# Attention scalars of a graph network: columns per group, or rows per pair of groups

## What is computed

```python
x = layernorm(x + gcn(x))                       # two graph convolutions, 128 -> 256 -> 128
xs, xd = x[src], x[dst]
att = sigmoid(xs @ W_att[:d] + xd @ W_att[d:] + b_att)
messages = (xs @ W_msg + b_msg) * att
aggregated = segment_sum(messages, dst, num_segments=num_nodes)
h = gru(aggregated, x)                          # W_ih, W_hh; then a batch norm over the nodes
return layernorm(x + h)
```

## Time and profile before

| | |
|---|---|
| median of 3 runs | 1699.89 us (1697.44 to 1700.52) |
| span of the profiled execution, all that is shown of its time | 1805.3 us |
| busy in it: PE, PEld | 1517.2 us (84%), 1054.6 us (58%) |
| busy in it: DVE, ACT, POOL | 1403.1 us (78%), 1172.9 us (65%), 986.4 us (55%) |
| HBM | 270.98 MB read, 175.92 MB written |

### The profile page before, as it was taken

One profiled execution on the slowest core, in us unless ns is written; L12 is line 12 of the kernel. 1 busy time (PEld: TensorE's weight loads), 2 busy tenths in 40 slices (PEclk: granted clock), 3 DMA queues, 4 the chain that ended last, 5 costly groups with the idle time before them and its releaser, 6 DMA issues.

```text
span 1805.3 us, 35081 instructions
## 1 busy us (share of the span) xinstructions
PE 1517.2 (84%) x7736; PEld 1054.6 (58%) x7736; DVE 1403.1 (78%) x4685; ACT 1172.9 (65%) x2896; POOL 986.4 (55%) x1014
## 2 busy tenths in 40 slices
PE   6303899999999938888888889999999999997764
PEld 3101677777777737767777776455555555555553
DVE  7827688888888847777677774788888888888897
ACT  6873455555555516666666665777777777776999
POOL 5002666666666356666656663666666666634443
PEclk9656999999999979999989998999999999999998
DMA  8898799988888737888766665877864445446997
GB/s 300 296 334 322 249 327 323 330 281 273 271 273 272 249 116 259 268 273 270 231 212 217 217 214 193 248 240 240 243 208 142 138 139 143 141 145 239 405 405 284
DMA packets 244030, 448.07 MB, mean 248 GB/s; under 512 B 39256, under 2 KB 40978, under 8 KB 243936
## 3 DMA queue, kind: packets, MB, share of 16 engines
q1 hardware_dynamic: 215248, 388.16, 62.3%
q0 software_dynamic: 28688, 58.89, 13.1%
HBM read 270.98 MB, written 175.92 MB: 248 GB/s over the span
## 4 chain that ended last, share of the span: by engine, by line
PE 46%; DVE 17%; issue 13%; ACT 10%; another core or an unknown queue 3%; DVEq 2%; DMA 1%; POOL 1%; ACTq 0%; SPq 0%; POOLq 0%
PE bank L1515 5%; PE bank L1523 5%; PE bank L1618 5%; PE bank L1605 5%; PE bank L1611 5%; PE bank L1607 5%; PE bank L1603 5%; PE bank L1610 4%; ACT page L905 4%; DVE page L1231 3%; ACT page L1008 3%; DVE gath L1397 3%; PE bank L1505 2%; PE bank L1549 2%
## 5 line engine op out<-in xcount | busy, mean ns | idle before, releaser
L783 POOL DMA_INDIRECT gath<-MT,ROWI x294 | 319.2, 1086 | 203.2 <-PE bank L1618 111.7
L783 POOL DMA_INDIRECT gath<-XP,ROWI x294 | 286.8, 976 | 228.6 <-remote 85.1
L783 POOL DMA_INDIRECT gath<-G,ROWI x294 | 278.8, 948 | 193.4 <-PE bank L1549 72.8
L879 ACT ACTIVATE page<-bank,b_sb 128x512 f32<-128x512 f32 x196 | 124.3, 687 | 164.5 <-remote 116.5
L1523 PEld LDWEIGHTS bank<-w_sb,page 128*128 128x128 f32 x1568 | 191.5, 192 | 51.5 <-issue 50.8
L1549 PE MATMUL bank<-gath,onehot 128*128 128x128 f32 x1176 | 168.4, 295 | 62.8 <-issue 30.5
L1523 PE MATMUL bank<-w_sb,page 128*128 128x128 f32 x1568 | 192.4, 275 | 4.2 <-issue 2.5
L1515 PE MATMUL bank<-page,w_sb 128*128 128x512 f32 x392 | 191.1, 610 | 3.6 <-DVE page L1212 2.8
L1549 PEld LDWEIGHTS bank<-gath,onehot 128*128 128x128 f32 x1176 | 149.2, 203 | 69.3 <-issue 64.9
L887 ACT ACTIVATE page<-bank,DINV 128x128 f32<-128x128 f32 x392 | 112.3, 372 | 74.9 <-remote 57.0
L905 ACT ACTIVATE page<-page,st_m,st_r 128x128 f32<-128x128 f32 x384 | 156.8, 479 | 0.0
(11 more groups left out here) (226 smaller groups left out, 3382.5 us busy)
## 6 DMA issues: line engine op xcount, KB each, us to landing
page<-YT SPq DMA_DIRECT2D x196, 256.0 KB, 7.9
MT<-page SPq DMA_DIRECT2D x98, 260.0 KB
XP<-page SPq DMA_DIRECT2D x98, 256.0 KB, 3.0
page<-in_xT SPq DMA_DIRECT2D x98, 256.0 KB
page<-DQ SPq DMA_DIRECT2D x98, 256.0 KB
G<-page SPq DMA_DIRECT2D x98, 256.0 KB
OWN<-page SPq DMA_DIRECT2D x98, 256.0 KB
page<-OWN SPq DMA_DIRECT2D x98, 256.0 KB
```

Of the source, the lines that this page charges most:

```text
L783: nc.gpsimd.indirect_dma_start(gath[k][:, w, 0:width], None, rows, bass.IndirectOffsetOnAxis(ap=ROWI[:, at:at + 1], axis=0)).then_inc(land ...
L879: last = nc.scalar.activation(rows[k], bank[2 + 2 * k + h][:], ACT.Relu, bias=b1_sb[:, h:h + 1])
```

## The change

For each group one product with the vectors as the stationary side, into two of four rows of a bank: `watt_pair[0]` has the vectors in columns 0 and 2, `watt_pair[1]` in columns 1 and 3, zeros elsewhere, and the two products of a pair of groups add up. So rows 0 and 1 hold the first scalar of the pair's groups, rows 2 and 3 the second. ACT copies the four rows to `att_rows` (two pages). SP stores rows 2 and 3 to AD. PE multiplies four rows by four columns of the identity per tile: one plain product for the first tile, which starts the bank anew, and three in transpose mode. DVE adds the bias on the way into the two `n_m` pages. MT is stored one step later (lag 9), and HN before it. The table `AD_ALL` goes, with its transposes, copy and stores at the end of the stage, and the four late recurrent products follow each other.

The core of the diff:

```diff
+        watt_pair = [sb(f"watt_pair{u}", [P, 4]) for u in range(2)]
...
-        AD_ALL = DSQ
+        att_rows = pages[16:18]
...
+                if (g := group_of(8)) and not g.kept:
+                    wait(sp, n_hk, g.done())
+                    sp.dma_start(group_of_table(HN, g), n_h[g.slot(4)]).then_inc(h_st[g.slot(4)], 16)
+                if (g := group_of(8)) and g.c % 2:
+                    wait(sp, n_ad, g.pair())
+                    sp.dma_start(AD[bass.ds(g.i * g.unroll + (g.c - 1), 2)].rearrange("a j p -> a (j p)"),
+                                 att_rows[g.pair_slot()][2:4, :]).then_inc(ad_st[g.pair_slot()], 16)
+                if g := group_of(9):
                     k = g.slot(8)
-                    wait(sp, n_mc, g.done())
+                    wait(sp, n_mc, g.pair())
                     sp.dma_start(group_of_table(MT, g), n_m[k][:]).then_inc(n_mst[k], 16)
...
-            sp.wait_ge(n_ad, 1)
-            whole = len(AD_CHUNKS) - 1
-            sp.dma_start(ad_rows[0:whole * P, :].rearrange("(q p) c -> p q c", p=P),
-                         n_h[3][:, 0:whole * P].rearrange("p (q c) -> p q c", c=P)).then_inc(ad_st, 16)
-            sp.dma_start(ad_rows[whole * P:NT, :], n_h[3][0:AD_CHUNKS[-1], whole * P:GN]).then_inc(ad_st, 16)
...
             def norm(group_of):
+                if (g := group_of(7)) and g.c % 2:
+                    k = g.pair_slot()
+                    wait(act, n_mm, g.pair())
+                    wait(act, ad_st[k], g.pair_dma_freed())
+                    nc.scalar.activation(att_rows[k][0:4, :], bank[4 + k][0:4, :], ACT.Copy).then_inc(n_ad, 1)
...
-            wait_all_dmas(act, h_st, 1, FREE)
-            act.wait_ge(n_adt, 1)
-            nc.scalar.activation(n_h[3], bank[3][:], ACT.Copy).then_inc(n_ad, 1)
...
+            for u in range(2):
+                nc.vector.memset(watt_pair[u][:], 0.0)
...
+            for u in range(2):
+                nc.vector.tensor_copy(watt_pair[u][:].rearrange("p (s u) -> p s u", s=2)[:, :, u:u + 1], watt_sb[:].unsqueeze(2))
...
-                    wait(dve, n_mm, g.done())
-                    nc.vector.tensor_copy(AD_ALL[:, bass.ds(g.index * J, J)], both[:, :, 1:2].rearrange("p j a -> p (j a)"))
-                    nc.vector.tensor_tensor(by_tile(n_m[g.slot(8)][:])[:, :, D:DM], both,
-                                            batt_sb[:].unsqueeze(1).to_broadcast([P, J, 2]), ALU.add).then_inc(n_mc, 1)
+                if (g := group_of(8)) and g.c % 2:
+                    wait(dve, n_adt, g.pair())
+                    both = bank[4 + g.pair_slot()][:, 0:4 * J].rearrange("p (j s u) -> p j s u", j=J, s=2)
+                    for u in range(2):
+                        last = nc.vector.tensor_tensor(by_tile(n_m[(g.c - 1 + u) % 8][:])[:, :, D:DM],
+                                                       both[:, :, :, u:u + 1].rearrange("p j s u -> p j (s u)"),
+                                                       batt_sb[:].unsqueeze(1).to_broadcast([P, J, 2]), ALU.add)
+                    last.then_inc(n_mc, 1)
...
-                    wait(pe, n_mc, g.freed(2))
+                    u = g.c % 2
+                    if u == 0:
+                        wait(pe, n_mc, g.pair_freed())
+                    product = nc.tensor.matmul(bank[4 + g.pair_slot()][0:4, :], watt_pair[u][:], y, start=u == 0, stop=u == 1)
+                    if u:
+                        product.then_inc(n_mm, 1)
+                if (g := group_of(7)) and g.c % 2:
+                    k = g.pair_slot()
+                    wait(pe, n_ad, g.pair())
                     for j in range(J):
-                        last = nc.tensor.matmul(bank[4 + g.slot(2)][:, 2 * j:2 * j + 2], y[:, j * P:(j + 1) * P], watt_sb[:], start=True, stop=True)
-                    last.then_inc(n_mm, 1)
+                        last = nc.tensor.matmul(bank[4 + k][:, 4 * j:4 * j + 4], att_rows[k][0:4, j * P:(j + 1) * P], ident[0:4, 0:4],
+                                                is_transpose=j > 0, start=True, stop=True)
+                    last.then_inc(n_adt, 1)
```

More of the change, by code:

```diff
@@ L115, in pairs, with pair, pair_slot, pair_freed @@
         return self.i * (self.unroll // 2) + (self.c + 1) // 2
+    def pair(self):
+        return self.i * (self.unroll // 2) + self.c // 2 + 1
+    def pair_slot(self):
+        return self.c // 2 % 2
+    def pair_freed(self):
+        return self.pair() - 2
+    def pair_dma_freed(self):
+        return self.i * (16 * self.unroll // 4) + 16 * (self.c // 4)
     def dma(self, k, n=1):
@@ L161, in in_register, with run_pass @@
     return value if isinstance(value, int) else eng.to_reg(value)
-def run_pass(eng, step, lag, kept_only=False, unroll=U):
+def run_pass(eng, step, lag, kept_only=False, unroll=U, head=None):
     def at(i, u, kept=None):
@@ L172, in at @@
         return group_of
-    first, border, last = -(-(lag + unroll) // unroll), FREE // unroll, NG // unroll
+    first, border, last = head or -(-(lag + unroll) // unroll), FREE // unroll, NG // unroll
     if not kept_only:
@@ L665, in norm @@
                     sp.dma_start(group_of_table(YT, g), n_T[k]).then_inc(n_yst[k], 16)
-                if g := group_of(8):
+                if (g := group_of(8)) and not g.kept:
[6 more added lines that the diff above has]
+                if g := group_of(9):
                     k = g.slot(8)
-                    wait(sp, n_mc, g.done())
+                    wait(sp, n_mc, g.pair())
                     sp.dma_start(group_of_table(MT, g), n_m[k][:]).then_inc(n_mst[k], 16)
[L670 to L674, removed]
+            run_pass(sp, norm, 9, unroll=8, head=2)
             sp.wait_ge(n_zz, NG)
@@ L687, in stored @@
                 wait_all_dmas(sp, n_mst)
-                sp.wait_ge(ad_st, 32)
+                for u in range(2):
+                    sp.wait_ge(ad_st[u], 16 * len(range(u, NG // 2, 2)))
                 wait_all_dmas(sp, h_st, 1, FREE)
@@ L911, in norm @@
                     wait(act, n_yst[k], g.dma_freed(4))
-                    wait(act, n_mm, g.freed(4))
+                    wait(act, n_mm, g.pair() - 2)
                     nc.scalar.activation(n_T[k], bank[2 + g.slot(2)][:], ACT.Copy).then_inc(n_trc, 1)
@@ L926, in hidden @@
                 nc.scalar.activation(kept(g) if g.kept else n_h[k], bank[6 + g.slot(2)][:], ACT.Copy).then_inc(n_hk, 1)
[L928 to L931, removed]
-            wait_all_dmas(act, h_st, 1, FREE)
-            act.wait_ge(n_adt, 1)
-            nc.scalar.activation(n_h[3], bank[3][:], ACT.Copy).then_inc(n_ad, 1)
-            for g in late[2:]:
+            run_pass(act, norm, 7, unroll=8)
+            for g in [Group(index // 8, index % 8, unroll=8) for index in range(LATE, NG)]:
                 hidden(g)
@@ L1566, in norm @@
                         recurrent(g)
-                    wait(pe, n_mc, g.freed(2))
+                    u = g.c % 2
[7 more added lines that the diff above has]
+                    wait(pe, n_ad, g.pair())
                     for j in range(J):
-                        last = nc.tensor.matmul(bank[4 + g.slot(2)][:, 2 * j:2 * j + 2], y[:, j * P:(j + 1) * P], watt_sb[:], start=True, stop=True)
-                    last.then_inc(n_mm, 1)
+                        last = nc.tensor.matmul(bank[4 + k][:, 4 * j:4 * j + 4], att_rows[k][0:4, j * P:(j + 1) * P], ident[0:4, 0:4],
+                                                is_transpose=j > 0, start=True, stop=True)
+                    last.then_inc(n_adt, 1)
             def norm_end():
-                late = [Group(index // 8, index % 8, unroll=8) for index in range(LATE, NG)]
-                pe.wait_ge(n_trc, NG)
-                for g in late[:2]:
+                for g in [Group(index // 8, index % 8, unroll=8) for index in range(LATE, NG)]:
                     recurrent(g)
[L1577 to L1584, removed]
+            both_ways(norm, 7, unroll=8, end=norm_end)
             pe.wait_ge(n_hk, NG)
@@ L1590, in gru @@
                 if g and g.fixed and g.index == 0 and mode is FAST:
-                    pe.wait_ge(n_ad, 1)
+                    pe.wait_ge(n_mc, NG // 2)
                     for k in range(2):
```

11 lines of the change are left out of this document (2 added, 9 removed).

## The result

| | before | after |
|---|---|---|
| median of 4 runs, us | 1698.71 (1697.44 to 1700.52) | 1725.36 (1724.41 to 1726.13) |
| ratio, 95% interval | | 1.0156 [1.0140, 1.0172] |
| the profiled execution: its time, its span, us | 1805.3 span; again, below: 1696.78, 1694.9 | 1725.16, 1723.0 |

The change costs 26.65 us. The forecast was 1716, the range 1674 to 1735, slower with 0.64: the side and the range hold, the size is 9 us short (16 us more than before were forecast).

A forecast was written before the change was run, and what follows sets the result against it. The prediction took PE to bound the norm loop at 3.54 us, gathers perhaps holding it to 3.75, base 3.65. Steady periods 12 us, others 3, stage end +1: +16 us, 1716 us, range 1674 to 1735.

The forecast's parts named there:

- I take this pace to be made by the recording itself: Norm and GCN loops: recording lets about 11.45 PE records per us through, so 4.48 us periods are shorter in the runs.
- The span of 1760: Profiled execution after the change: 45 records a group at 11.45 per us, 3.93 us a period, a span of about 1760.
- the rival of a real pace: Norm loops: the recorded pace holds in the runs too, so the change makes the kernel faster, 1656 us; chance 0.12.
- The base of 3.65: Norm loop before: a period of 3.65 us in the runs, between PE's 3.54 and the gathers' 3.75.
- PE's period of 3.88: Norm loop after: aggregation 1.45, transposes 0.44, recurrent product 0.86, row product 0.86, small passes 0.27, together 3.88 us a group.
- The sum of 0.23 a group: Norm loop: 0.23 us more a group, 12 us for 53 periods, 3 us for 29 others at half.
- The end of the stage, +1: End of the norm stage: between -2 and +2 us, taken as +1 for the early loads of YT.
- The 4-row passes: Five small passes back to columns: between nearly nothing and 0.53 us a pair; 0.53 taken, 0.27 a group.
- ScalarE, VectorE and SyncE at no cost: Norm loop: row copy, addition and stores on these engines stay covered by PE's 3.88 us period and cost nothing.
- Cheap passes by four stationary columns: Row product: passes cost by their stationary columns, 0.2 us, PE's period 3.1, up to 25 us faster, 1675; chance 0.06.
- A new wait at each pair: Norm loop: PE stands for a late row copy, 0.58 plus 0.2 us a pair, 32 us on top, 1748; chance 0.04.
- Hidden: Norm loop: the period is already 3.85 or more, PE's 0.34 goes into slack, 1700 give or take 3; chance 0.18.

The follow-up runs named there:

- e4: The kernel before with two gathers per group in the norm stage in place of three: 1667.97 us, ratio 0.9816 to before.
- e1: The kernel before, no edit, profiled a second time: 1696.78 us (one run).
- e8: e2 with the 4-row products replaced by four 128 x 128 transposes of all rows of the bank: 1701.29 us, ratio 1.0024 to before.
- e2: The changed kernel with the row product's stationary side padded by zeros from 4 to 128 columns: 1712.41 us, ratio 1.0080 to before.
- e9: e8 with two gathers per group in the norm stage in place of three: 1688.78 us, ratio 0.9930 to before.

## Why the prediction was right in side and short in size

**What bounds the kernel.** PE's 3.54 us were right (3.53 in e4). "I take this pace to be made by the recording itself" was wrong: e1 and after were recorded too, and their spans are 2 us under their runs' times. The span of 1760 that came out of it fell with it; it is 1723.0. What the step was used for, a loop that is faster in the runs than 4.48, was right, but for another reason: that one execution was itself slower than the runs, and what held it is open. So the rival of a real pace is out. The rule of the Trainium skill's "Runtime: NRT & Kernel Launch" (the ~15µs preamble/postamble breakdown) that was weighed there puts a profile's total some 6 us above the reported time. The spans here lie 2 us below it, 1723.0 against 1725.16; whether the page's total is this span, no run shows.

**The base of 3.65,** the middle between PE's 3.54 and the gathers' 3.75, was mis-sized: it is the upper end, 3.76. The rows for it were there (three times 1.25 us), and for the middle spoke only the 105.4 us by which that one execution stood over the runs.

**PE's period of 3.88** was mis-sized: 4.03. The row product's 0.86 is 0.95, the small passes' 0.53 is 0.49, and the aggregation's 1.45, taken as untouched, is 1.53. The two terms that are short, by 0.09 each, have one cause, loads that no longer run beside the passes ahead: the step priced each product by rows in which all neighbours have its shape.

**The sum of 0.23 a group** has both errors in it, and they work against each other: 4.03 - 3.76 = 0.27. That 0.23 came so near is in part luck. The prediction counted 82 of the 97 periods and halved 29 of them for busy DMA engines, 12 + 3 us. From the first aggregation of the stage to the last it is 390.80 us in after (616.49 to 1007.29) and 367.05 in e1 (616.50 to 983.55), 23.8 us more. From group 11 on it is 347.09 against 323.94, 0.27 for each of 86 periods. The 29 periods from group 11 to 40 take 117.03 us in after (660.20 to 777.23) and 110.13 in e1 (659.61 to 769.74): 6.9 more, 0.24 each, where the halving has 3. So no halving is seen.

**The end of the stage, +1,** was too small. PE's timeline in e1 (start, us, engine, line, instruction, in brackets the idle time before it): the first and the last aggregation, the last recurrent products (L1538), the first early GRU product (L1594), the first GRU aggregation (L1618):

```profile
616.50 2.90 PE L1549 MATMUL bank<-gath,onehot 128*128 128x128 f32 x12 [11.23 <-DMA gath<-G,ROWI]
...
983.55 1.58 PE L1549 MATMUL bank<-gath,onehot 128*128 128x128 f32 x12
...
1001.79 1.88 PE L1538 MATMUL bank<-page,whh_sb 128*128 128x512 f32 x4
...
1007.72 1.73 PE L1594 MATMUL bank<-page,whh_sb 128*128 128x512 f32 x2 [4.05 <-issue]
...
1012.93 1.03 PE L1618 MATMUL bank<-onehot,gath 128*128 128x172 f32 x6
```

And in after, where L1552, L1609 and L1633 are the same lines of products and L1591 the last 4-row passes:

```profile
616.49 2.90 PE L1563 MATMUL bank<-gath,onehot 128*128 128x128 f32 x12 [10.69 <-DMA gath<-G,ROWI]
...
1007.29 1.60 PE L1563 MATMUL bank<-gath,onehot 128*128 128x128 f32 x12
...
1025.13 0.57 PE L1591 MATMUL bank<-ident,page 4*128 4x4 f32 x5 [0.68 <-ACT page L914]
...
1025.63 3.80 PE L1552 MATMUL bank<-page,whh_sb 128*128 128x512 f32 x8
...
1034.69 2.04 PE L1609 MATMUL bank<-page,whh_sb 128*128 128x512 f32 x2 [5.27 <-issue]
...
1040.41 1.03 PE L1633 MATMUL bank<-onehot,gath 128*128 128x172 f32 x6
```

From the last aggregation of the stage to the first of the GRU it is 29.38 us in e1 and 33.12 in after, 3.7 more. To the end of the recurrent products it is 2.0 more: the last small passes wait 0.68 us for their row copy and begin only at 1025.13, and the recurrent products come behind them. The idle time ahead of the GRU's first product is 1.2 longer, which stays open, and the early products take 0.5 more. With 23.8 in the stage that makes 27.5 of the 28.1 us between the two spans.

**The 4-row passes:** of 0.53 and nearly nothing the upper end was right (0.49). The weight loads of after by shape, in 650 to 950 us (line, records, then busy us, mean ns, idle time ahead) show the rule that was weighed:

```profile
L1552 PEld LDWEIGHTS bank<-page,whh_sb 128*128 128x128 f32 x148 | 22.4, 192 | 0.0
L1591 PEld LDWEIGHTS bank<-ident,page 4*128 4x128 f32 x185 | 17.7, 171 | 31.9 <-issue 31.9
L1584 PEld LDWEIGHTS bank<-page,watt_pair 128*4 128x4 f32 x148 | 6.7, 84 | 56.1 <-issue 56.1
```

A load of 4 rows and 128 columns takes 171 ns in the mean, near the 192 of 128 x 128, one of 128 rows and 4 columns 84: by columns and not by rows, as "TensorE: Matmul & The Clock Gate" (LDWEIGHTS) of the Trainium skill has it.

**ScalarE, VectorE and SyncE at no cost:** right in the loop, whose chain in after holds PE alone. VectorE's relief was worth nothing either, as it bounded nothing.

**The rivals.** Cheap passes by four stationary columns: no, the row product costs what its 512 streamed columns cost, and more. A new wait at each pair: not in the loop's chain, once at the end. Hidden: true of the first 0.23 us a group, PE's room in the kernel before (e4), into which e8's 0.18 goes; the change needs 0.50.

## What to carry to other kernels

Price a new product with its neighbours: here a matmul of another shape than those around it also left its own first load and that of the next product outside (0.09 us each), and padding with zeros to the full shape took both back (e2, e9). Before costing an addition on a busy engine, find which engine ends the period; here a full PE in one stretch hid that a gather queue with 0.23 us a group more paced the loop. And when one profile stands 6% over the runs it belongs to, take its durations, but not its pace.

## What the runs showed of the hardware that was not expected

- A stationary side of 4 or 64 columns among ones of 128 is slower than one of 128 (0.95 and 1.00 against 0.86 for the same 512 columns streamed in two passes), and slows the next product by 0.09 to 0.19.
- An aggregation of 12 passes takes 1.34 us behind a product that streams 512 columns in the same shape (e2) or behind four transposes (e9), and 1.45 behind the eight passes that stream two columns each (e4). That such short passes leave its first loads no room is argued, not tested.
- Ahead of the first GRU product PE is idle for 4.05 us in e1 and 5.27 in after, with no wait that the profile shows; what the entry into the next stage spends there is open.
